# Last stage's shared network: three fp32r products each, or one fp32 product of the raw weights

## The reference, cut to what matters

```
x = x + attention(x, cond)
x = x + gated_recurrence(x, cond)
out = sum over the two chosen experts e of w[b, e] * mask[e] * (gelu(x @ ew1[e] + eb1[e]) @ ew2[e] + eb2[e])
shared = gelu(x @ sw1 + sb1) @ sw2 + sb2        # 256 -> 1024 -> 256, every token
x = x + out + shared
h[t] = tanh(x[t] @ Wx + b + h[t-1] @ Wh)        # t = 0..255, h[-1] = cond
x = x + h
```

## Time and profile before

| | us |
|---|---|
| median of 3 runs | 1307.96 |
| profiled execution | 1305.88 |
| its span | 1304.1 |
| TensorE busy | 1216.4 (93%) |
| VectorE busy | 879.0 (67%) |
| ScalarE busy | 623.2 (48%) |
| GpSimd busy | 333.9 (26%) |

### The profile page before, as it was taken

The page is one execution under the profiler, slowest core; times in us unless marked ns, Lnnn a source line. Parts: engine busy times, 40 slices in busy tenths (PEclk is TensorE's granted clock), DMA queues, the critical chain, the costliest instruction groups (busy, mean ns, idle before and its releaser), DMA issues. The chain is left out here.

```text
span 1304.1 us, 34455 instructions
## 1 busy us (share of the span) xinstructions
PE 1216.4 (93%) x14104; PEld 961.0 (74%) x14104; DVE 879.0 (67%) x2047; ACT 623.2 (48%) x1168; POOL 333.9 (26%) x311
## 2 busy tenths in 40 slices
PE   3789999999999988499999999999999999999995
PEld 2456666766665433159999999999978888888883
DVE  6788888888775889957666666666655555555552
ACT  2377777777777879433333333333323333333331
POOL 1436566465552679600000000000010000000000
PEclk9699999999999999799999999999999999999995
DMA  9013242332212100059999999999900000000000
GB/s 359 3 50 99 85 136 74 123 99 86 87 50 82 64 1 1 0 203 397 378 368 360 368 363 371 365 366 361 370 11 19 11 19 11 20 11 19 11 19 18
DMA packets 82507, 190.39 MB, mean 146 GB/s; under 512 B 4144, under 2 KB 15536, under 8 KB 82096
## 3 DMA queue, kind: packets, MB, share of 16 engines
q1 hardware_dynamic: 82352, 188.21, 40.2%
HBM read 162.76 MB, written 25.17 MB: 144 GB/s over the span
## 5 line engine op out<-in xcount | busy, mean ns | idle before, releaser
L1417 ACT ACTIVATE g<-ph,b 128x256 f32<-128x256 f32 x256 | 121.6, 475 | 247.9 <-PE ph L1606 247.8
L693 DVE TENSOR_REDUCE mx<-pR 128x4 f32<-128x1024 f32 x128 | 156.4, 1225 | 62.7 <-PE pR L899 61.4
L1825 DVE STREAM_TRANSPOSE preT<-pr 128x64 f32<-128x64 f32 x256 | 63.9, 250 | 157.7 <-PE pr L1720 155.7
L1800 ACT ACTIVATE hs<-preT 128x32 f32<-128x32 f32 x256 | 58.8, 230 | 217.2 <-DVE preT L1825 217.0
L1526 DVE CAST ghi<-g 128x256 fp32r<-128x256 f32 x256 | 74.8, 292 | 128.2 <-ACT g L1417 128.0
L1622 PE MATMUL py<-ghi,w 128*128 128x256 f32 x512 | 145.7, 285 | 1.7 <-DVE glo L1528 1.6
L1604 PE MATMUL ph<-xhi,w 128*128 128x256 f32 x512 | 145.3, 284 | 0.0
L1605 PE MATMUL ph<-xlo,w 128*128 128x256 f32 x512 | 144.9, 283 | 0.0
L1623 PE MATMUL py<-glo,w 128*128 128x256 f32 x512 | 144.9, 283 | 0.0
L1624 PE MATMUL py<-ghi,w 128*128 128x256 f32 x512 | 144.9, 283 | 0.0
L1606 PE MATMUL ph<-xhi,w 128*128 128x256 f32 x512 | 144.9, 283 | 0.0
(11 more groups left out here) (226 smaller groups left out, 2898.1 us busy)
## 6 DMA issues: line engine op xcount, KB each, us to landing
w<-weight_halves SPq DMA_DIRECT2D x132, 1024.0 KB, 8.0
weight_halves<-wparts SPq DMA_DIRECT2D x40, 512.0 KB, 3.9
modw<-in_ew SPq DMA_DIRECT2D x32, 256.0 KB, 4.5
xn<-in_x_tok SPq DMA_DIRECT2D x4, 1024.0 KB, 11.8
XT<-in_x_dm SPq DMA_DIRECT2D x2, 2048.0 KB, 14.6
out_dm<-raw SPq DMA_DIRECT2D x16, 256.0 KB, 2.0
modw<-in_sw SPq DMA_DIRECT2D x8, 256.0 KB, 4.5
raw<-in_sw SPq DMA_DIRECT2D x2, 1024.0 KB, 7.7
```

Of the source, the lines that this page charges most:

```text
L693: nc.vector.reduce_max(mx[:, :, 2 * j:2 * j + 2].rearrange("p t s -> p s t"), pR[k][:].rearrange("p s (t k) -> p s t k", t=TC), AX.X).then ...
L1417: nc.scalar.activation(g[:, t % RING], ph[t % RING][:, 0:T], ACT.Gelu_apprx_tanh, bias=b1[:, n, f:f + 1]).then_inc(gelu_done, 1)
```

## The change

The shared network's weights are no longer split: the pieces are 32 instead of 40 (three in rounds 0 and 1, then two), weight_halves has one expert less, and the load of its halves at the end of the experts is gone. The last stage uses raw1 and raw2 themselves, in plain fp32 products with x and with the gelu's result, so one product stands for three. For that x must be whole: GpSimd adds xhi and xlo for each chunk into `xf` (two buffers). XT itself can't serve, as the experts' results have been added to it. VectorE's `split` is gone, and the down products read the gelu's result directly, from a ring of 4 (`KEEP`). The quota is 2 products a step, and 1 in each step with k mod 16 = 14 from step 16 on; nothing is done ahead of step 0. y0 moves from raw1 to a free part of wfih_sb, for which ScalarE waits for b1 before the copy; `staged` and `g` get buffers of their own; w1 and w2 end with the experts; GpSimd's loop over the chunks is written out.

```diff
-            return max(0, 2 * (r + 1) + min(r + 1, 10))
+            return max(0, 2 * (r + 1) + min(r + 1, 2))
...
-PIECES = 8 * (NE + 1)
+PIECES = 8 * NE
...
-        y0 = raw1[:, :, 0:FIRST * T]
+        room = env["wfih_sb"][:].rearrange("p c n -> p (c n)")
+        y0 = room[:, 0:DC * FIRST * T].rearrange("p (c n) -> p c n", c=DC)
...
-                load_weights(sp, JOBS, halves[NE:NE + 1], up_done, down_done)
...
                 act.wait_ge(down_first, FC)
+                act.wait_ge(b1_ready, 1)
                 nc.scalar.copy(y0, py[0][:, :, 0:FIRST * T]).then_inc(y_kept, 1)
-                act.wait_ge(b1_ready, 1)
...
-    ITEMS = 6
-    AHEAD = 12
+    ITEMS = DC
+    KEEP = 4
...
-            taken = AHEAD
+            taken = 0
...
         def quota(k):
 
-            if k < CH:
-                return (4, 6, 5, 6)[k % 4]
-            return (5 if k % 2 == 0 else 7) - (k % 8 in (2, 3))
+            return 1 if k >= CH and k % CH == 14 else 2
...
+            def ffn(c):
+
+                pe.wait_ge(xf_ready, c - FIRST + 1)
                 for n in range(FC + 2):
                     if n < FC:
                         pe.wait_ge(gelu_ok, FC * (c - FIRST) + n + 1)
                         for k in range(DC):
-                            whi, wlo = (w1[:, BUF, v, k, n * P:(n + 1) * P] for v in range(2))
-                            dst = ph[n % RING][:, 0:N]
-                            nc.tensor.matmul(dst, whi, xhi[:, k][xs], start=(k == 0), stop=False)
-                            yield
-                            nc.tensor.matmul(dst, whi, xlo[:, k][xs], start=False, stop=False)
-                            yield
-                            i = nc.tensor.matmul(dst, wlo, xhi[:, k][xs], start=False, stop=(k == DC - 1))
+                            i = nc.tensor.matmul(ph[n % RING][:, 0:N], raw1[:, k, n * P:(n + 1) * P], xf[:, c % 2, k],
+                                                 start=(k == 0), stop=(k == DC - 1))
                             if k == DC - 1:
                                 i.then_inc(up_ok, 1)
                             yield
                     if n >= 2:
                         f = n - 2
-                        pe.wait_ge(lo_ok, FC * (c - FIRST) + f + RING + 1)
+                        pe.wait_ge(gelu_ok, FC * (c - FIRST) + f + RING + 1)
                         if f == 0 and c > FIRST:
                             pe.wait_ge(x_ready, c)
...
                         for m in range(DC):
...
+                            i = nc.tensor.matmul(py[:, m, 0:N], raw2[:, f, m * P:(m + 1) * P], g[:, f % KEEP],
+                                                 start=(f == 0), stop=(f == FC - 1))
...
-                    act.wait_ge(lo_ok, FC * (c - FIRST) + f + 1)
+                    act.wait_ge(down_ok, FC * (c - FIRST) + f + 1)
...
-            def split(c, f):
...
+            def whole_x(c):
+                if c >= FIRST + 2:
+                    pool.wait_ge(up_ok, FC * (c - 1 - FIRST))
+                at = slice(CH * c, CH * (c + 1))
+                nc.gpsimd.tensor_tensor(xf[:, c % 2], xhi[:, :, :, at].bitcast(fp32), xlo[:, :, :, at].bitcast(fp32), ALU.add).then_inc(xf_ready, 1)
...
+            whole_x(FIRST)
+            whole_x(FIRST + 1)
+            for c in range(NCH):
+                stage(c)
+                if c + FIRST + 2 < NCH:
+                    whole_x(c + FIRST + 2)
```

More of the change, by code:

```diff
@@ L132, in build @@
         pieces_out = [sem(hold, f"pieces_out{q}") for q in range(2)]
-        halves = nc.dram_tensor("weight_halves", (NE + 1, 2, P, 2, DC * F), fp32).ap()
+        halves = nc.dram_tensor("weight_halves", (NE, 2, P, 2, DC * F), fp32).ap()
         def vec(name, a=None, z=None):
@@ L1332, in experts @@
         with ExitStack() as routed:
+            w1 = sb(routed, "w1", [P, 2, 2, DC, F], fp32r)
+            w2 = sb(routed, "w2", [P, 2, 2, FC, D], fp32r)
             g = sb(routed, "g", [P, RING, T])
@@ L1640, in shared_and_rnn @@
     XT, out = env["XT"], env["out"]
-    xhi, xlo, w1, w2, wx, wh = (ex[k] for k in ("xhi", "xlo", "w1", "w2", "wx_sb", "wh_sb"))
+    xhi, xlo, raw1, raw2, wx, wh = (ex[k] for k in ("xhi", "xlo", "raw1", "raw2", "wx_sb", "wh_sb"))
     N = B * CH
-    BUF = TOP * B % 2
     QD = 4
@@ L1697, in down_step @@
             return step_of(FFN * (c + 1 - FIRST))
-        gelus_in, splits_in, adds_in = ({k: [] for k in range(-1, T)} for _ in range(3))
+        gelus_in, adds_in = ({k: [] for k in range(T)} for _ in range(2))
         for c in range(FIRST, NCH):
             for f in range(FC):
[L1702 to L1706, removed]
+                gelus_in[up_step(c, f)].append((c, f))
+            adds_in[down_step(c) + 1].append(c)
         def half(k):
@@ L1769, in all_ffn @@
                 for c in range(FIRST, NCH):
-                    yield from ffn(c, (slice(None), slice(0, B), slice(CH * c, CH * (c + 1))))
+                    yield from ffn(c)
             pe.wait_ge(ex["wxh_in"], 32)
-            for w in range(2):
-                for h in range(2):
-                    pe.wait_ge(ex["w_in"][w][h][BUF], 16 * (TOP * B // 2 + 1))
             work = all_ffn()
-            for _ in range(AHEAD):
-                next(work, None)
             pe.wait_ge(row1_set, 1)
@@ L1801, in recur @@
                                      ACT.Tanh).then_inc(h_ready, 1)
-            for k in range(-1, T):
-                if k >= 0:
-                    recur(k)
+            for k in range(T):
+                recur(k)
                 for c, f in gelus_in[k]:
                     act.wait_ge(up_ok, FC * (c - FIRST) + f + 1)
-                    act.wait_ge(lo_ok, FC * (c - FIRST) + f + 1)
-                    nc.scalar.activation(g[:, f % RING], ph[f % RING][:, 0:N], ACT.Gelu_apprx_tanh,
+                    act.wait_ge(down_ok, FC * (c - FIRST) + f + 1)
+                    nc.scalar.activation(g[:, f % KEEP], ph[f % RING][:, 0:N], ACT.Gelu_apprx_tanh,
                                          bias=vec("sb1", f, f + 1)).then_inc(gelu_ok, 1)
@@ L1839, in add_x @@
                 if c >= FIRST:
-                    dve.wait_ge(down_ok, FC * (c + 1 - FIRST) + RING)
+                    dve.wait_ge(down_ok, FC * (c + 1 - FIRST) + KEEP)
                 dve.wait_ge(staged_done[s], 2 * PRIMED + 2 * (c // 2))
@@ L1848, in add_x @@
                     i.then_inc(half_added if m == 0 else x_ready, 1)
-            for k in range(-1, T):
-                if k >= 0:
-                    recur(k)
+            for c in range(FIRST):
+                add_x(c)
+            bias_of_state()
+            for k in range(T):
+                recur(k)
                 for c in adds_in[k]:
                     add_x(c)
-                if k < 0:
-                    for c in range(FIRST):
-                        add_x(c)
-                    bias_of_state()
-                for c, f in splits_in[k]:
-                    split(c, f)
         @block.gpsimd
@@ L1874, in stage @@
                                             hs[:, s, e::2, :, half(e + 1)], ALU.add).then_inc(staged_done[s], 1)
-            with pool.Fori(0, NCH // 2) as i:
-                stage(i, 0)
-                stage(i, 1)
+            whole_x(FIRST)
[4 more added lines that the diff above has]
+                    whole_x(c + FIRST + 2)
         @block.sync
@@ L1883, in _ @@
                 sp.sem_inc(out_done[s], 16 * PRIMED)
-            for signal in (gelu_ok, lo_ok, down_ok):
-                sp.sem_inc(signal, RING)
+            sp.sem_inc(gelu_ok, RING)
+            sp.sem_inc(down_ok, KEEP)
             def send(q, s):
```

37 lines of the change are left out of this document (10 added, 27 removed).

## The result

The changed kernel takes 1344.27 us (median of 4 runs, 1343.56 to 1345.68). The kernel before, run beside it, takes 1307.68 us (4 runs, 1307.33 to 1310.51). The ratio is 1.0276, with an interval of 1.0258 to 1.0294: slower by 36.6 us, where 35 were forecast (1343 us, range 1336 to 1353). The profiled execution took 1344.59 us with a span of 1342.4, against 1305.88 and 1304.1: 38.3 us more span.

What follows compares the result with a forecast made beforehand. TensorE's queue was taken to bound the last stage. Steps and tail +34.1 us, opening +1 and -0.25, sum +35 on the profiled 1305.9 gives 1340.9; 2.1 more for the median gives 1343 us, range 1336 to 1353.

Steps and rivals of the forecast that it cites:

- What bounds the stage: Last stage: a step's time is the sum queued on TensorE; the h chain is shorter, 1.06 us a step.
- The price of a product: Network products on TensorE: one fp32 product costs 0.43 us against 0.36 for three fp32r; 31 us over 448.
- Four passes at the fp32r pitch: Rival on network products: an fp32 product costs 0.48 us, +22 us, total 1365 us; chance 6%.
- two records at that pitch: Rival on network products: two records at 0.12 us make a product 0.24 us, total 1258 us; chance 3%.
- Steps: Last stage, step 0 to 231: 347.5 us, with steps of 1.66 (even), 1.40 (odd) or 1.23 us (one product).
- The tail: Bare steps 231 to 255: 29.8 us instead of 25.9, with the clock at half about 5.3 us after the products.
- VectorE, gelu, whole x: Last stage: casts and subtractions removed, gelu's new place and GpSimd's additions each 0 us; first addition at most 0.3.
- Weight pieces: Attention: eight of 40 weight pieces no longer split and stored, 0 us, bounds -1 and +1.
- The opening: Start of the last stage: step 0 may start 0.25 us sooner; TensorE's idle time may halve the clock, 1 us.
- The half clock: Start of the last stage: half clock after TensorE's idle time for at most 4 us, taken as 1 us, bounds 0 to 2.
- Ahead of the last stage: Before the last stage: fewer weight pieces, y0's copy waiting for b1, and the shared halves' load gone: 0 us each.
- The third rival: Network products: weight loads set the pitch, 0.24 us a product, steps above the chain on average, 1258 us; chance 3%.

Runs made afterwards that it cites:

- e1: Changed kernel with each network product as a single fp32r pass instead of an fp32 product, on stand-in weights: 1243.99 us, ratio 0.9512.
- e6: Changed kernel with three network products in even steps and one in odd ones instead of two and two: 1351.62 us, ratio 1.0328.
- e4: Changed kernel without GpSimd's whole-x additions, TensorE reading XT in their place: 1342.91 us, ratio 1.0273.
- e7: Kernel before, with the cast of the gelu's output done twice on VectorE: 1312.09 us, ratio 1.0029.
- e5: Changed kernel with the eight pieces of the shared weights split and stored in the attention again, though nobody reads them: 1344.58 us, ratio 1.0269.
- e8: Kernel before, with unread fp32r products filling TensorE's idle time in the tail's bare steps: 1303.25 us, ratio 0.9953.
- e10: The kernel of e8 run again, beside e9 on the same chip, against the kernel before: 1303.36 us, ratio 0.996.
- e9: e8's kernel with the bias rows moved ahead of the products that run before step 0, and 18 of these instead of 12: 1305.82 us, ratio 0.9982.
- e2: Changed kernel with six unread fp32 products added between the bias rows and the first drive: 1344.14 us, ratio 1.0284.
- e3: Changed kernel with the copy of cond into hs on ScalarE instead of VectorE: 1343.59 us, ratio 1.0277.

## Why the prediction was right

- **What bounds the stage.** TensorE's queue, not the chain. Shown three times: no wait of TensorE in the changed kernel's steps of 1.42 and 1.65 us; an even step with one product takes 1.21 us, with two 1.65, both above the chain's 1.06; and in e1 and e6 the chain takes over where the queue is shorter.
- **The price of a product.** 0.43 us, from the projection's rows. A product more or less in a run changes a step by 0.43 (e6) to 0.44 us. This term is 31 us of the loss. Four passes at the fp32r pitch (0.48) and two records at that pitch (0.24) are both refuted by it. The Trainium skill, page "FP8 and Floating Point Precision", section "TensorE Precision Notes", counts four passes for fp32. The trace does not speak against the count: at the granted clock of 1.00 (2.4 GHz) 0.43 us are 1032 cycles, 4.03 for each of the 256 columns. What failed in that rival is the price of a pass: an fp32r product at 0.12 us is 1.13 cycles a column, so its pitch is more than a quarter of an fp32 product. That a record is two passes is not shown.
- **Steps.** 347.5 us forecast for step 0 to 231, 350.2 measured. Of the 2.7 over, 1.95 are steps 0 and 1 at half clock (5.01 us instead of 3.06), for which 1 was taken. The other 0.8 are 0.0035 us in each of the remaining steps: the odd step is 1.42 us where 1.40 was forecast, the even one 1.65 where it was 1.66.
- **The tail.** 29.8 forecast, 29.88 measured, with the clock at 0.94 from 1312 to 1313 us and at 0.50 after, so it fell some 5.6 us after the last product. Two small misses cancel here: step 232 takes 1.27 us, as the last chunk's addition stands ahead of its transpose, and step 236 is only in part at half clock (1.19 us).
- **VectorE, gelu, whole x.** 0 forecast. But for one weight load (0.2 us) no row of the steps shows TensorE waiting for any of them, and e4 and e1 confirm it. e7 adds that the cover was thin on the other side: more VectorE work would have cost a little.
- **Weight pieces.** 0 forecast, and e5 shows 0.
- **The opening.** The one step that came out with the wrong sign: "step 0 may start 0.25 us sooner" was 0.85 us later. The prediction gave GpSimd's first addition a cost only through TensorE's wait for its result. It held VectorE: the copy of 128x32 that step 0 waits for took 1.22 us beside the addition, not 0.18, and without it step 0 is 1.04 us sooner (e4). The half clock was priced at 1 us with 0 to 2 as bounds, and was 1.95 in the profiled execution. That it comes from the dropped 12 products is **not** shown: e7, e8 and e10, with those products in place, show 0.50 in steps 0 and 1 too, which then take 4.35 us, and the profiled execution of the kernel before, with 1.00 there and 2.82 us, was the exception. This fits the medians, which differ by 36.6 us where the two profiled executions differ by 38.7, but the clock of unprofiled runs is not known. What decides it stays open.
- **Ahead of the last stage.** 0.66 us later, of which 0.38 were there at 88.9 us, before anything changed: scatter between executions. The clearing of `hs` starts anywhere from 950.5 to 957.5 us in the profiled executions.
- **The third rival's sum.** It called steps of 1.28 and 1.02 us "above the chain on average". e6 shows that steps do not average: the odd ones would have stood at the chain's 1.06, some 5 us more than its 1258.
- **How near the number came.** 36.6 us between the medians, 35 forecast. Span against span it is 38.3: the opening, its clock, the steps and the later start add 3.5 us that were not forecast. The forecast also added 2.1 us from the profiled execution to the median, but the changed kernel's profiled execution (1344.59, where 1340.9 was forecast) is 0.3 above its median. So the mechanism and the 31 us hold by the rows; that the medians agree within 2 us is in part luck.

## What to carry to other kernels

On an engine that never waits, the price of a change is the count of instructions times their pitch in this kernel, plus the first weight load of each run: one fp32 product in place of three fp32r ones is 0.43 us against 0.36, however much work it takes off the others. A step costs the longer of its work on the full engine and its chain, so work has to be balanced step by step, not only in sum. And where that engine's work runs out ahead of the chain, look at its granted clock: filling its idle time in the tail brought 5 us here, 3.5 of them seen in the steps. An order that is written from a count of steps (e9) has to be looked at again when the count moves: an addition one step earlier cost 1.5 us.

## What the runs showed of the hardware

- A small VectorE copy took 1.22 us (128x32, fp32, from SBUF to SBUF) when it was issued beside a GpSimd addition of 128x512, and 0.18 alone (e4). It ended at 956.08, about when the first of the two additions did. The next copy, out of PSUM and beside the second addition, took 0.21 us. The Trainium skill, page "SBUF — State Buffer", section "SBUF: two separate sides", calls the port pair that VectorE and GpSimd share an exclusive lock: of a GpSimd instruction and a VectorE one in a two-port mode, whichever starts first holds it for its whole instruction. The trace agrees: the addition started at 954.79 and the copy at 954.86, and on ScalarE the same copy took 0.22 us beside the same addition (e3).
- The granted clock fell to 0.50 at the opening of the stage even where TensorE was already in dense products (from 953.25 in e2, from 954.04 in e9), each time after 1.76 us without work and the bias rows. It stayed there for 3.4 us in both, and for 6.8 in the changed kernel. Two executions with the same code up to there can differ in it: 1.00 throughout in the kernel before, 0.50 in e8.
- In the tail it fell 5 to 6 us after the last product of the network. Until then TensorE did only the steps' own products (busy 2.58 us from 1307.3 to 1312.8 in the changed kernel, at clock 1.00). It did not fall with that idle time filled (e8). A bare step is 1.06 us at 1.00 and 1.29 at 0.50.
- Executions whose code is the same up to the last stage reach it at different times: the clearing of `hs` starts at 952.36 in the kernel before and at 957.49 in e8. No run here shows the cause.
